# Window attention with MLP and GDN: value projection and value copies moved ahead of the turns, and another strip for odd halves

## The chip, the cores and the metric

One core of a Trainium2 chip runs the whole program. The metric is the device time of one execution in microseconds (us). TensorE (PE in the rows) multiplies matrices, VectorE (DVE) and ScalarE (ACT) do elementwise work, GpSimd (POOL) some more of it, SyncE (SP) issues the transfers by DMA. Each engine works through its own list of instructions in order; semaphores make one wait for another.

## What is computed

The input x is 4 images of 96 channels and 128 x 128 points. The reference is a shifted-window transformer block followed by a generalised divisive normalisation:

```
y   = layernorm(x) over channels, rolled by (-4, -4), cut into windows of 8 x 8 = 64 tokens
q, k, v = y @ qkv_w.T + qkv_b, in 6 heads of 16
out = softmax(q k^T / 4 + mask) v @ proj_w.T + proj_b, windows put back, rolled by (4, 4)
x   = x + out
x   = x + gelu(layernorm(x) @ mlp_w1.T + mlp_b1) @ mlp_w2.T + mlp_b2
out = x * rsqrt(gamma_eff @ x^2 + beta_eff) over channels
```

The mask (-100) concerns the windows that the roll has wrapped: the last window of each row of windows, and all windows of the last row of an image.

## The kernel before

A unit is a row of 16 windows (8 image rows, 1024 tokens); there are 64 units. Each is worked on in two halves of 8 windows, so there are 128 halves, A = 0 to 127; the odd half of a unit holds windows 8 to 15, and so the masked last window. A half has four pairs of windows (pair 3 is LAST). All engines run the same pipeline of rounds H: in each round the stage of a step works on half H + offset. TURN_IN = 4 and TURN_OUT = 3 prepare later halves, QK = 1 and ATTEND = 0 are attention, PROJECT = -2, MLP = -3, UP = -4, SETTLE = -5 and DIVIDE = -6 are the steps behind it. The order of the steps in a round is written out by hand in one function `steps` for each engine.

Layout. Many tiles have 96 channels or heads as three groups of 32 partitions; partitions 96 to 127 are a fourth strip. So that all 128 partitions work on 384 columns (MAIN) instead of 96 on 512, the fourth pair's columns of the three groups are laid side by side in the strip. `in_strips` does a projection in this way: three matmuls of 384 columns for the main pairs, three of 128 for the strip.

One round on TensorE, for the half H of attention: `scores(H)` (four row groups; the strip's scores, group GROUPS = 3, go to pv_bank, the others to the three score_banks), `project_k` and `project_q` of H+1, `times_v(H-1)` (probabilities times values, into pv_bank), `denominators(H-6)`, `sum_probs(H-1)`, `project(H-2)`, `mlp_down(H-5)`, then `turn_run(H)`: the turns (transposes) of the probabilities of H, mixed with those of the normalised tokens y1 of H+3 and y2 of H-3 into turn_banks; then `project_v(H)` (8 matmuls of 96 columns into pv_bank), `mlp_up` parts 0 and 1 of H-4, `turn_in` of x for H+4 and of x2 for H-2 (turned to tokens, into turn_banks), `mlp_up` part 2.

VectorE: maxima and shifts of the scores (the strip's group first, then 0, 1, 2, with maxima and shifts interleaved), `normalise` for y1 and y2, `first_residual`, `divide(H-1)` (reads pv_bank, writes attended), `second_residual`, `outputs`, `split_y2(H-3)` (the rounding rest of y2), `v_blocks(H)` (four copies from pv_bank to v_block), `statistics` of x and x2 out of turn_banks, `variances`. ScalarE: table load, copies of k and q, the exponentials, with logarithms and inverses between them, table load, `y2_copy`, `y1_copy` out of turn_banks, then copies of the turned probabilities and gelus. SyncE issues the loads of x, the stores, and moves between strip and groups (`move_attended`, three transfers a half).

pv_bank is used in turn by the strip's scores of H, by times_v of H-1, and by project_v of H. The waits that matter around the change:

```
times_v(A):   pe.wait_ge(scores_shifted, softmax_count(A + 1, GROUPS))
project_v(A): wait(pe, attended_ready, A)
turn_in(A):   wait(pe, y_ready[0], min(H + TURN_OUT + 1, HALVES))
              wait(pe, y2_split, min(H + MLP + 1, HALVES))
split_y2(A):  dve.wait_ge(y_ready[1], A + 1), and y_ready[0] of the same round
scores(A):    waits for probs_t_ready and v_ready of the half before, q_ready, keys_copied
```

mlp_up part 2 waits for the gelu of part 0, whose bank of PSUM it takes over. The masks are added by matmuls of 4 rows (L1045) behind the scores of the window pair they belong to.

Of the kernel before, what the change touches and what calls it, by code (L numbers as in the profile page):

```python
# [32 lines left out]
HALF = UNIT // 2  # L33
HALVES = 2 * UNITS
HALF_WINDOWS = WINDOWS // 2
# [32 lines left out]
def window_block(nc, x, qmask, kmask, ident, head_mask, ones_pair, norm1_w, norm1_b, qkv_t, qkv_b,  # L68
# [8 lines left out]
    with ctx:  # L77
# [151 lines left out]
        def wait(engine, semaphore, count):  # L229

            if count > 0:
                engine.wait_ge(semaphore, count)
# [26 lines left out]
        def mm_bank(name, A):  # L259
            return mm_banks[MM_PLACE[name, A] % len(mm_banks)]  # L260
# [43 lines left out]
        def norm_round(A, ln):  # L304

            return A - (TURN_OUT, MLP)[ln]

        SOFTMAX_ORDER = (GROUPS, 0, 1, 2)

        def softmax_count(A, g):  # L310
# [3 lines left out]
        def group(j, width=32):  # L314
            return slice(width * j, width * (j + 1))
# [7 lines left out]
        def _(sp):  # L323
# [46 lines left out]
            def move_attended(A):  # L370

                wait_alone(sp, attended_ready, A + 1)
                for j in range(HEAD_PAIRS):
                    sp.dma_start(attended[group(j), MAIN:HALF], attended[strip, group(j, 128)])\
                        .then_inc(attended_moved, 16)

            def move_x3(A):
# [125 lines left out]
        def _(act):  # L503
# [55 lines left out]
            def softmax_exp(A, g):  # L559
                act.wait_ge(scores_shifted, softmax_count(A, g))  # L560
                for bank in ((0, 1, 2) if g == GROUPS else (0, 1) if g < 2 else (2,)):
                    wait(act, probs_turned[bank], A)
                dst = probs[:, :, LAST, :, :] if g == GROUPS else probs[:, g, 0:LAST, :, :]
                nc.scalar.activation(dst, shifted[:, g, :, :].rearrange("t (i e) k -> t i e k", e=TILE_HEADS),  # L564
                                     ACT.Exp).then_inc(probs_ready, 1)

# [70 lines left out]
        def _(dve):  # L637
# [166 lines left out]
            def divide(A):  # L804
                dve.wait_ge(inv_sum_ready, A + 1)
                dve.wait_ge(pv_made, A + 1)
                wait(dve, proj_made, A)
                nc.vector.tensor_tensor(attended[:, 0:MAIN], pv_bank[:, 0:MAIN], inv_sum[:, :],
                                        ALU.mult).then_inc(attended_ready, 1)

            def first_residual(A):
# [22 lines left out]
            def steps(run, H):  # L834

                run(max_scores, ATTEND, GROUPS)
                run(shift_scores, ATTEND, GROUPS)
                run(max_scores, ATTEND, 0)
                run(max_scores, ATTEND, 1)
                run(shift_scores, ATTEND, 0)  # L840
                run(max_scores, ATTEND, 2)
                run(shift_scores, ATTEND, 1)
                run(shift_scores, ATTEND, 2)
                run(normalise, TURN_OUT, 0)
                run(normalise, MLP, 1)
                run(first_residual, PROJECT)
                run(divide, ATTEND - 1)
                run(second_residual, SETTLE)
                run(outputs, DIVIDE)
                run(split_y2, MLP)  # L850
                run(v_blocks, ATTEND)
                run(statistics, TURN_IN, 0)
                run(statistics, PROJECT, 1)
                variances(H)
                if H == -TURN_IN:
                    fold_qkv()
                if H == -TURN_IN + 1:
                    fold_mlp()
                if H == -TURN_IN + 2:
                    split_mlp()  # L860
# [5 lines left out]
        def _(pe):  # L866
# [80 lines left out]
            def turn_run(H):  # L947
# [30 lines left out]
                for p in range(PAIRS):  # L978
                    if has(norm2):
                        turn_normed(norm2, 1, p, 0)  # L980
                    if has(A):
                        made = turn_windows(A, 2, p, 1)
                        if p == PAIRS - 1:
                            made.then_inc(probs_turned[2], 1)

            def project_k(A):

                if A == 0:
                    pe.wait_ge(weights_folded, 10)
                    pe.wait_ge(cleared, 2)  # L990
                pe.wait_ge(y_ready[0], A + 2 - A % 2)
                mm_wait("k", A)
                in_strips(mm_bank("k", A), wk, y1_windows(A, 0, 2 * LAST), y1_windows(A, 2 * LAST))\
                    .then_inc(k_made, 1)

            def project_q(A):

                pe.wait_ge(y_ready[0], A + 2 - A % 2)
                mm_wait("q", A)
                in_strips(mm_bank("q", A), wq, y1_windows(A, 0, 2 * LAST), y1_windows(A, 2 * LAST))\  # L1000
                    .then_inc(q_made, 1)

            def project_v(A):

                wait(pe, attended_ready, A)
                for p in range(PAIRS):
                    made = nc.tensor.matmul(pv_bank[:, p * DIM:(p + 1) * DIM], y1_windows(A, 2 * p, 2 * p + 2),  # L1007
                                            wv[:, :], start=True, stop=True)
                made.then_inc(v_made, 1)
# [5 lines left out]

            def window_of(A, r, i, n):

                return (A % 2) * HALF_WINDOWS + 2 * (LAST if r == GROUPS else i) + n

            def scores(A):  # L1020

# [28 lines left out]
            def times_v(A):  # L1050

                pe.wait_ge(v_ready, A + 1)
                pe.wait_ge(probs_t_ready, GROUPS * (A + 1))
                if has(A + 1):
                    pe.wait_ge(scores_shifted, softmax_count(A + 1, GROUPS))
                for turn in range(2 * LAST):
                    at, n = turn // 2, turn % 2
                    first = turn * TOKENS
                    for s in range(STRIPS):
                        m, p = (s, at) if s < HEAD_PAIRS else (at, LAST)  # L1060
                        made = nc.tensor.matmul(pv_bank[group(s), first:first + TOKENS],  # L1061
                                                v_block[:, (A % 2) * HALF_WINDOWS + 2 * p + n, m, :],
                                                probs_t[:, A % 2, m, p, n * TOKENS:(n + 1) * TOKENS],
                                                start=True, stop=True)
                made.then_inc(pv_made, 1)

            def sum_probs(A):

                if has(A + 1):
                    pe.wait_ge(scores_shifted, softmax_count(A + 1, 0))  # L1070
                for m in range(HEAD_PAIRS):
                    nc.tensor.matmul(sum_bank[group(m), 0:MAIN], ones_pair_sb[:, :],
                                     probs_t[:, A % 2, m, 0:LAST, :], start=True, stop=True)
                for m in range(HEAD_PAIRS):
                    made = nc.tensor.matmul(sum_bank[strip, group(m, 128)], ones_pair_sb[:, :],  # L1075
                                            probs_t[:, A % 2, m, LAST, :], start=True, stop=True)
                made.then_inc(sums_made, 1)

            def project(A):
# [40 lines left out]
            def steps(run, H):  # L1120
# [6 lines left out]
                run(sum_probs, ATTEND - 1)  # L1127
                run(project, PROJECT)
                run(mlp_down, SETTLE)
                turn_run(H)  # L1130
                run(project_v, ATTEND)
                run(mlp_up, UP, 0)
                run(mlp_up, UP, 1)
                run(turn_in, TURN_IN, 0)
# [62 lines left out]
```

## Time and profile before

| | before |
|---|---|
| median of 3 runs | 1757.68 us (1756.24 to 1758.75) |
| the profiled execution, its own time | 1756.11 us |
| span of its trace | 1754.3 us |
| TensorE busy (matmul / weight load) | 1662.1 us (95%) / 1464.1 us (83%) |
| ScalarE busy | 1487.8 us (85%) |
| VectorE busy | 1423.0 us (81%) |
| GpSimd busy | 361.1 us (21%) |
| granted TensorE clock, mean | 0.991 of full speed |
| the chain that ended last, by engine | PE 71%, DVE 17%, issue 5%, ACT 5% |

The busy shares are means over the whole span. A matmul is pipelined: the next one starts before it ends, so the pace of a row of matmuls is read from start to start. The chain is followed back from the last instruction, at each step to what released it.

### The profile page before, as it was taken

The numbers are of one execution on the slowest core, as the hardware profiler recorded it, in microseconds if no ns is written. First come the engines' busy times: TensorE is split into PE (matmuls) and PEld (weight loads), VectorE is DVE, ScalarE is ACT, GpSimd is POOL, SyncE is SP. The second block draws the span as 40 slices with busy tenths as digits, with TensorE's granted clock in tenths as the row PEclk, the third lists the DMA queues.
The fourth block names the chain that finished last, engine by engine and source line by source line (L and its number), as shares of the span: only waits on it lengthen the run. The fifth ranks groups of instructions, "written<-read, shape, count | busy, mean of one in ns | idle before, by whom it ended". The sixth has DMA issues, their size and how long they took to land.

```text
span 1754.3 us, 83088 instructions
## 1 busy us (share of the span) xinstructions
PE 1662.1 (95%) x33524; PEld 1464.1 (83%) x33524; DVE 1423.0 (81%) x4142; ACT 1487.8 (85%) x2957; POOL 361.1 (21%) x459
## 2 busy tenths in 40 slices
PE   5899999999999999999999999999999999999995
PEld 3688888888888888888888888888888888888874
DVE  5788888888888888888888888888888888888871
ACT  2688888888888888888888888888888888888884
POOL 2121221221221221221221221221222222222111
PEclk9999999999999999999999999999999999999997
DMA  2112122122122122122122122122121222222111
GB/s 57 47 51 64 55 61 62 54 64 59 55 61 62 54 61 62 54 67 57 54 69 56 53 68 57 53 68 57 55 66 56 56 66 57 57 64 57 46 34 32
DMA packets 179169, 100.38 MB, mean 57 GB/s; under 512 B 26868, under 2 KB 178790, under 8 KB 178790
## 3 DMA queue, kind: packets, MB, share of 16 engines
q1 hardware_dynamic: 178228, 94.96, 19.5%
q8 instruction: 269, 4.41, 1.1%
q14 instruction: 110, 0.90, 0.2%
q10 hardware_dynamic: 562, 0.11, 0.0%
HBM read 32.05 MB, written 25.17 MB: 33 GB/s over the span
## 4 chain that ended last, share of the span: by engine, by line
PE 71%; DVE 17%; issue 5%; ACT 5%; DMA 1%; SPq 0%; POOL 0%; DVEq 0%; POOLq 0%
PE mm_bank L906 10%; PE mm_bank L1111 10%; PE mm_bank L1096 8%; PE score_banks L936 7%; PE pv_bank L1061 6%; PE mm_bank L904 6%; DVE stats L721 5%; PE mm_bank L1108 5%; PE pv_bank L1007 4%; DVE v_block L783 4%; PE turn_banks L942 4%; PE score_banks L1075 3%; PE score_banks L1037 3%; DVE row_max L792 2%; DVE shifted L799 2%
## 5 line engine op out<-in xcount | busy, mean ns | idle before, releaser
L514 ACT ACT_TABLE_LOAD x256 | 328.4, 1283 | 4.6
L564 ACT ACTIVATE probs<-shifted 128x384 f32<-128x384 f32 x512 | 265.7, 519 | 32.0 <-DVE shifted L799 29.0
L1108 PE MATMUL mm_bank<-hidden,w 128*32 128x384 f32 x2304 | 277.4, 492 | 0.1
L1111 PE MATMUL mm_bank<-hidden,w 128*32 128x128 f32 x2304 | 276.8, 275 | 0.0
L593 ACT ACTIVATE hidden<-mm_bank 128x512 f32<-128x512 f32 x384 | 238.4, 621 | 42.2 <-PE mm_bank L1096 41.5
L1111 PEld LDWEIGHTS mm_bank<-hidden,w 128*32 128x32 f32 x2304 | 254.4, 111 | 1.2
L469 POOL TENSOR_TENSOR x<-x,b_bias 128x384 f32<-128x384 f32 x128 | 105.7, 826 | 716.7 <-PE turn_banks L928 716.7
L770 DVE TENSOR_TENSOR y_lo<-turn_banks,y_hi 96x512 fp32r<-96x512 f32 x128 | 87.9, 687 | 197.2 <-ACT y L538 194.3
L575 ACT ACTIVATE probs_t<-score_banks 128x512 f32<-128x512 f32 x384 | 220.1, 617 | 0.0
L792 DVE TENSOR_REDUCE row_max<-score_banks 128x6 f32<-128x384 f32 x384 | 199.4, 547 | 0.0
L799 DVE TENSOR_TENSOR shifted<-score_banks,row_max 128x384 f32<-128x384 f32 x384 | 199.3, 546 | 0.0
L721 DVE BATCH_NORM_STATS2 stats<-turn_banks 128x6 f32<-128x96 f32 x1024 | 181.7, 249 | 17.1 <-PE turn_banks L923 11.2
L783 DVE COPY v_block<-pv_bank 64x192 f32<-64x192 f32 x512 | 180.4, 352 | 11.7 <-PE pv_bank L1007 6.5
L936 PE MATMUL score_banks<-ident_sb,probs 64*128 64x64 f32 x3072 | 181.8, 229 | 4.0 <-ACT probs L564 2.3
L1096 PE MATMUL mm_bank<-y_hi,w_hi 97*128 97x512 f32 x384 | 172.9, 450 | 0.1
L936 PEld LDWEIGHTS score_banks<-ident_sb,probs 64*128 64x128 f32 x3072 | 146.5, 138 | 30.0 <-issue 24.4
L1061 PEld LDWEIGHTS pv_bank<-probs_t,v_block 128*32 128x32 f32 x6144 | 97.2, 110 | 74.6 <-issue 74.1
L1061 PE MATMUL pv_bank<-probs_t,v_block 128*32 128x64 f32 x6144 | 114.3, 221 | 44.4 <-DVE shifted L799 40.5
L1096 PE MATMUL mm_bank<-y_lo,w_hi 97*128 97x512 f32 x384 | 152.0, 396 | 0.0
L1096 PE MATMUL mm_bank<-y_hi,w_lo 97*128 97x512 f32 x384 | 150.6, 392 | 0.0
L1037 PE MATMUL pv_bank<-k_block,q 32*64 32x128 f32 x1536 | 147.5, 284 | 0.0
L1007 PE MATMUL pv_bank<-wv,y 97*128 97x96 f32 x1024 | 145.8, 286 | 0.0
(110 smaller groups left out, 4568.1 us busy)
## 6 DMA issues: line engine op xcount, KB each, us to landing
x_ext<-in_x SPq DMA_DIRECT2D x128, 192.0 KB, 3.2
k_block<-k SPq DMA_DIRECT2D x256, 96.0 KB, 2.0
out<-o_ext SPq DMA_DIRECT2D x64, 192.0 KB, 2.8
x_ext<-in_x SPq DMA_DIRECT2D x128, 48.0 KB, 2.8
attended<-attended SPq DMA_DIRECT2D x384, 16.0 KB, 1.8
x<-x SPq DMA_DIRECT2D x384, 16.0 KB, 1.8
out<-o_ext SPq DMA_DIRECT2D x64, 96.0 KB, 2.6
out<-o_ext SPq DMA_DIRECT2D x128, 48.0 KB, 2.1
```

Source lines behind the costliest of these rows:

```text
L514: nc.scalar.preload_act_table_set(name)
L564: nc.scalar.activation(dst, shifted[:, g, :, :].rearrange("t (i e) k -> t i e k", e=TILE_HEADS), ACT.Exp).then_inc(probs_ready, 1)
L593: nc.scalar.activation(hidden[:, n, :], mm_bank(f"mlp1_{n}", A)[:, :], ACT.Gelu)\
L721: made = nc.vector.bn_stats(stats[:, (H + 1) % 2, ln, n, :], chunk)
L783: made = nc.vector.tensor_copy(to, values[:, :, :, e, :])
L792: nc.vector.tensor_reduce(row_max[:, g, :], group_scores(g), op=ALU.max, axis=AX.X)\
L799: nc.vector.tensor_tensor(shifted[:, g, :, :], group_scores(g), row_max[:, g, :].unsqueeze(2) .broadcast_to([128, LAST * TILE_HEADS, TOKENS]),
L936: return nc.tensor.transpose(score_banks[:, bank, first:first + TOKENS], probs[half, m, p, :, :], ident_sb[half, half])
L1061: made = nc.tensor.matmul(pv_bank[group(s), first:first + TOKENS], v_block[:, (A % 2) * HALF_WINDOWS + 2 * p + n, m, :], probs_t[:, A % 2, ...
L1096: made = nc.tensor.matmul(mm_bank(f"mlp1_{n}", A)[:, :], w[:, cols], tokens, start=part == 0, stop=part == 2)
L1108: nc.tensor.matmul(to[group(j), 0:MAIN], w2[:, n, group(j)], hidden[:, n, 128:HALF], start=first, stop=last)
L1111: made = nc.tensor.matmul(to[strip, group(n, 128)], w2[:, c, group(n)], hidden[:, c, 0:128], start=c == 0, stop=c == HID_CHUNKS - 1)
```

## The change

On TensorE `project_v` is run before `turn_run` instead of behind it, and it also waits for the shift of the strip's scores of its own half. On VectorE `v_blocks` is run before `split_y2` instead of behind it. And the pair of windows that is laid in the fourth strip is no longer pair 3 in every half: in odd halves it is pair 0, and the three main pairs are 1 to 3 (`main_pairs`, `side_pair`). Slices that followed from the old choice follow from the new one: the columns of attended, the slices of the probabilities, the windows of q and k, the places of the masks.

```diff
@@ -305,6 +305,22 @@
+        def main_pairs(A):
+            return range(A % 2, A % 2 + LAST)
+        def side_pair(A):
+            return 0 if A % 2 else LAST
+        def main_tokens(A):
+            return slice(A % 2 * 128, A % 2 * 128 + MAIN)
+        def side_tokens(A):
+            return slice(side_pair(A) * 128, side_pair(A) * 128 + 128)
         SOFTMAX_ORDER = (GROUPS, 0, 1, 2)
...
@@ -371,7 +387,8 @@
                 for j in range(HEAD_PAIRS):
-                    sp.dma_start(attended[group(j), MAIN:HALF], attended[strip, group(j, 128)])\
+                    first = main_tokens(A).start + 128 * j
+                    sp.dma_start(attended[group(j), side_tokens(A)], attended[strip, first:first + 128])\
                         .then_inc(attended_moved, 16)
...
@@ -560,7 +577,8 @@
                     wait(act, probs_turned[bank], A)
-                dst = probs[:, :, LAST, :, :] if g == GROUPS else probs[:, g, 0:LAST, :, :]
+                pairs = slice(main_pairs(A)[0], main_pairs(A)[-1] + 1)
+                dst = probs[:, :, side_pair(A), :, :] if g == GROUPS else probs[:, g, pairs, :, :]
                 nc.scalar.activation(dst, shifted[:, g, :, :].rearrange("t (i e) k -> t i e k", e=TILE_HEADS),
...
@@ -805,7 +823,7 @@
                 wait(dve, proj_made, A)
-                nc.vector.tensor_tensor(attended[:, 0:MAIN], pv_bank[:, 0:MAIN], inv_sum[:, :],
+                nc.vector.tensor_tensor(attended[:, main_tokens(A)], pv_bank[:, 0:MAIN], inv_sum[:, :],
                                         ALU.mult).then_inc(attended_ready, 1)
...
@@ -847,8 +865,8 @@
                 run(outputs, DIVIDE)
+                run(v_blocks, ATTEND)
                 run(split_y2, MLP)
-                run(v_blocks, ATTEND)
                 run(statistics, TURN_IN, 0)
...
@@ -983,6 +1001,11 @@
+            def qk_windows(A):
+                side = 2 * side_pair(A)
+                return y1_windows(A, 2 * main_pairs(A)[0], 2 * main_pairs(A)[-1] + 2), y1_windows(A, side, side + 2)
             def project_k(A):
...
@@ -990,18 +1013,19 @@
                 mm_wait("k", A)
-                in_strips(mm_bank("k", A), wk, y1_windows(A, 0, 2 * LAST), y1_windows(A, 2 * LAST))\
+                in_strips(mm_bank("k", A), wk, *qk_windows(A))\
                     .then_inc(k_made, 1)
...
                 mm_wait("q", A)
-                in_strips(mm_bank("q", A), wq, y1_windows(A, 0, 2 * LAST), y1_windows(A, 2 * LAST))\
+                in_strips(mm_bank("q", A), wq, *qk_windows(A))\
                     .then_inc(q_made, 1)
...
+                pe.wait_ge(scores_shifted, softmax_count(A, GROUPS))
                 wait(pe, attended_ready, A)
...
@@ -1015,7 +1039,7 @@
-                return (A % 2) * HALF_WINDOWS + 2 * (LAST if r == GROUPS else i) + n
+                return (A % 2) * HALF_WINDOWS + 2 * (side_pair(A) if r == GROUPS else main_pairs(A)[i]) + n
...
@@ -1057,7 +1081,7 @@
                     for s in range(STRIPS):
-                        m, p = (s, at) if s < HEAD_PAIRS else (at, LAST)
+                        m, p = (s, main_pairs(A)[at]) if s < HEAD_PAIRS else (at, side_pair(A))
                         made = nc.tensor.matmul(pv_bank[group(s), first:first + TOKENS],
...
@@ -1070,10 +1094,10 @@
                     nc.tensor.matmul(sum_bank[group(m), 0:MAIN], ones_pair_sb[:, :],
-                                     probs_t[:, A % 2, m, 0:LAST, :], start=True, stop=True)
+                                     probs_t[:, A % 2, m, main_pairs(A)[0]:main_pairs(A)[-1] + 1, :], start=True, stop=True)
                 for m in range(HEAD_PAIRS):
                     made = nc.tensor.matmul(sum_bank[strip, group(m, 128)], ones_pair_sb[:, :],
-                                            probs_t[:, A % 2, m, LAST, :], start=True, stop=True)
+                                            probs_t[:, A % 2, m, side_pair(A), :], start=True, stop=True)
                 made.then_inc(sums_made, 1)
...
@@ -1127,8 +1151,8 @@
                 run(mlp_down, SETTLE)
+                run(project_v, ATTEND)
                 turn_run(H)
-                run(project_v, ATTEND)
                 run(mlp_up, UP, 0)
...
```

## Rows read from the trace of the kernel before

**Rows 1.** Busy time of each engine in an even and an odd round.

```profile
core 0: us, PE busy (x) PEld busy (x) DVE busy (x) ACT busy (x) POOL busy (x), PEclk, DMA share, GB/s
803.50:816.60 13.10, 12.43 (x259) 11.01 (x258) 10.99 (x32) 11.68 (x24) 3.74 (x5) 1.00 0.24 66
816.60:829.70 13.10, 13.03 (x265) 11.61 (x264) 10.98 (x32) 11.52 (x24) 1.82 (x2) 1.00 0.20 58
```

**Rows 2.** Matmuls of times_v (L1061) in 113 rounds: durations, first and last start.

```profile
L1061 PE MATMUL pv_bank<-probs_t,v_block x5424: 215/219/244, 156.2 to 1624.7; 128*32 128x64 f32 x194
```

**Rows 3.** Waits of the whole span: us in total, times, longest.

```profile
DVE y_lo L770 <- ACT y L538: 194.3, 122, 2.0
...
ACT y_hi L544 <- PE turn_banks L942: 75.3, 127, 1.2
...
ACT hidden L593 <- PE mm_bank L1096: 41.5, 130, 2.1
PE pv_bank L1061 <- DVE shifted L799: 40.5, 61, 1.3
ACT probs L564 <- DVE shifted L799: 29.0, 67, 1.0
```

**Rows 4.** Timeline of VectorE: start, us, line, operation, idle before.

```profile
802.82 0.54 DVE L808 TENSOR_TENSOR attended<-pv_bank,inv_sum 128x384 f32<-128x384 f32 x1
...
804.07 0.55 DVE L830 TENSOR_TENSOR o_ext<-x,inv_den 128x384 f32<-128x384 f32 x1
806.20 0.69 DVE L770 TENSOR_TENSOR y_lo<-turn_banks,y_hi 96x512 fp32r<-96x512 f32 x1 [1.58 <-ACT y L538]
806.80 1.45 DVE L783 COPY v_block<-pv_bank 64x192 f32<-64x192 f32 x4
808.28 1.42 DVE L721 BATCH_NORM_STATS2 stats<-turn_banks 128x6 f32<-128x96 f32 x8
...
811.12 0.56 DVE L799 TENSOR_TENSOR shifted<-pv_bank,row_max 128x384 f32<-128x384 f32 x1
...
819.30 0.69 DVE L770 TENSOR_TENSOR y_lo<-turn_banks,y_hi 96x512 fp32r<-96x512 f32 x1 [1.59 <-ACT y L538]
```

**Rows 5.** Timeline of ScalarE in the even round.

```profile
804.96 0.59 ACT L544 ACTIVATE y_hi<-turn_banks 96x512 fp32r<-96x512 f32 x1 [0.57 <-PE turn_banks L942]
...
806.93 0.62 ACT L593 ACTIVATE hidden<-mm_bank 128x512 f32<-128x512 f32 x1
```

**Rows 6.** Timeline of TensorE in the even round.

```profile
803.48 0.77 PE L936 MATMUL score_banks<-ident_sb,probs 64*128 64x64 f32 x17
...
804.73 0.22 PE L936 MATMUL score_banks<-ident_sb,probs 64*128 64x64 f32 x1
804.89 1.13 PE L1007 MATMUL pv_bank<-wv,y 97*128 97x96 f32 x8
805.80 0.48 PE L1096 MATMUL mm_bank<-y_hi,w_hi 97*128 97x512 f32 x1
...
807.28 0.49 PE L923 MATMUL turn_banks<-ident_sb,x_ext 96*128 96x96 f32 x4
...
807.86 0.47 PE L1096 MATMUL mm_bank<-y_hi,w_hi 97*128 97x512 f32 x1
...
808.72 0.35 PE L1037 MATMUL score_banks<-k_block,q 32*64 32x128 f32 x6
...
809.63 0.52 PE L904 MATMUL mm_bank<-y,wk 97*32 97x384 f32 x3
...
811.83 0.88 PE L1061 MATMUL pv_bank<-probs_t,v_block 128*32 128x64 f32 x48 [0.67 <-DVE shifted L799]
```

**Rows 7.** Timeline of TensorE in the odd round.

```profile
820.94 0.48 PE L1096 MATMUL mm_bank<-y_hi,w_hi 97*128 97x512 f32 x1
...
821.82 0.35 PE L1037 MATMUL score_banks<-k_block,q 32*64 32x128 f32 x6
...
823.32 0.52 PE L904 MATMUL mm_bank<-y,wk 97*32 97x384 f32 x3
...
824.91 0.31 PE L1061 MATMUL pv_bank<-probs_t,v_block 128*32 128x64 f32 x6
```

## The prediction

> **What bounds the kernel now.** I read the page first: no engine is idle for long, TensorE least of all. So the question is which loop of waits sets the length of a round, and the views of one pair of rounds tell it. The busy time of the two rounds from 803.5 to 829.7 us [rows 1] shows TensorE at 12.43 of 13.10 us in the even round and 13.03 in the odd one. The 113 rounds (5424 / 48 matmuls) in the middle of the trace have their first product with the values at 156.2 and their last at 1624.7 us [rows 2]: 1468.5 / 112 = 13.1 us a round, so these two stand for all. ScalarE works 11.68 and 11.52, VectorE 10.99 and 10.98. TensorE is full in odd rounds and has 0.67 us to spare in even ones.
>
> The list of waits [rows 3] says what that spare time is: in 61 rounds, one in two, TensorE waits at the products with the values (L1061) for VectorE's shifted scores, 40.5 us in all. VectorE waits 194.3 us for the copies of y (122 times, 1.59 us each) and ScalarE 75.3 us for the turns (127 times, 0.59 each). Put in order of time [rows 4 to 7], that is one loop through three engines. The last turn ends at 804.73 + 0.22 = 804.95. ScalarE starts at 804.96 with the copy of y2, then copies y1. VectorE, idle since 804.62, splits y2 from 806.20 to 806.89, copies the values (v_block, to 808.25), takes the statistics (808.28), the variances, the maximum and the shift of the fourth strip's scores (to 811.68). TensorE waits for that and starts times_v at 811.83, goes on through denominators, sums, project and mlp_down without a pause, and turns again. From the split's end to times_v it takes 811.83 - 806.89 = 4.94 us, and in the odd round 824.91 - 819.99 = 4.92. Both rounds are as long as this loop; the value projection (804.89) runs beside ScalarE's copies and is not on it.
>
> **The change, step by step.** *Loss: the value projection enters the loop.* project_v now stands between mlp_down and the turns. Its eight matmuls take 0.91 us from their first start to the first start of mlp_up behind them (804.89 to 805.80), and 1.13 from first start to last end [rows 6]. The turns, both copies of y and the split come later by something between these; I take the middle, 1.02. What could cover it is a wait that the turns now have, and I see none: they start right behind mlp_down (803.48), and ScalarE, the next in the loop, is waiting for them in each round.
>
> The rows also show what a change of tile costs on TensorE: from the last turn (64 rows) to the first value matmul (97 rows) 0.16 us pass from start to start. The Trainium skill (TensorEngine Tiling (Array Packing), Key Properties) has a rule that speaks against this change: going to another tiling mode drains the engine. Before, a round goes from 32-column tiles to 64-row turns to the whole array; afterwards to the whole array, back to the turns and to the whole array again, one switch more. By that rule with the row's 0.16 the loss would be 1.18 instead of 1.02; no row of this case shows the step from values to turns.
>
> *Its waits.* project_v now waits for the shift of the fourth strip (already met, since times_v waited for it) and, earlier than before, for the division of the half before, since both use pv_bank. The division ends at 802.82 + 0.54 = 803.36 [rows 4]; with the 0.15 us that TensorE took behind the shift (811.68 to 811.83) the values could start at 803.51, where the turns started at 803.48. So it costs nothing but has no slack: whatever is queued behind it on TensorE (turns, mlp_up, turn_in) and ScalarE's copies would be late with it.
>
> *Gain: the value copies leave the loop.* v_blocks now stands ahead of the split. The values are ready by about 803.48 + 1.13 = 804.61, VectorE's outputs end at 804.62, so the four copies (1.45 us) run from 804.65 to 806.1, while the split must wait until 806.20 + 1.02 = 807.22 in any case. VectorE's idle time hides them with 1.1 us to spare; without that they would hold up the split and the statistics queued behind it.
>
> But the statistics need more than VectorE: turn_in waits for the split (y2_split), and the statistics read what turn_in wrote. Before, turn_in (807.28 to 807.77) was done while VectorE copied values. Now it stands in the loop: split's end + 0.15 + the 0.49 of the first four turns + 0.01 (as ScalarE behind the last turn) = 0.65 after the split, where the statistics now start 1.39 after it (808.28 - 806.89). From the statistics to times_v nothing changes, 3.55. Split to times_v becomes 4.20 instead of 4.94: gain 0.74. The 0.15 is bounded by 0 and by the 0.39 that passed with TensorE still busy (806.89 to 807.28), so the gain by 0.50 and 0.89.
>
> *TensorE's own way to times_v* is now nearly as long. mlp_up's third part waits for the first gelu, which ends at 807.55 [rows 5], 0.66 after the split, + 0.15 = 0.81 after it (turn_in alone would let it start at 0.15 + 0.58 = 0.73). In an even round, from there 809.63 - 807.86 = 1.77 to the keys and 824.91 - 823.32 = 1.59 to times_v: 4.17, just under VectorE's 4.20. In an odd round the scores take 823.32 - 821.82 = 1.50, against 809.63 - 808.72 = 0.91 in an even one [rows 6, 7]: 0.59 for the mask matmuls, which stand in one row group.
>
> *The strip.* Taking pair 0 as the strip of odd halves moves the masked last window from the strip to the three main pairs, so its three masks fall on three row groups instead of one. Number and shape of matmuls, copies, exponentials and moves by DMA stay. Between nothing and all of the 0.59 can be saved; I take two thirds, 0.39, because three row groups share it (the scores of four groups already overlap: 48 matmuls in 0.91). The odd way becomes 0.81 + (824.91 - 820.94) - 0.39 = 4.39 instead of 4.92: 0.53 gained. With nothing saved 4.78 (0.14 gained), with all of it 4.19, and VectorE's 4.20 decides.
>
> *ScalarE* gets the turns 1.02 later but times_v only 0.3 to 0.5 later, so its softmax comes late by 0.5 to 0.7 against TensorE. It has 0.30 of wait before the third gelu (41.5 us in all) and 0.44 before an exponential (29.0 us) to take that up [rows 3]; I put the rest at nothing.
>
> *Sum.* Even round 1.02 - 0.74 = +0.28; odd 1.02 - 0.53 = +0.49; mean 0.385. The loop with all its parts stands in halves 3 to 123, 121 rounds (before that there is no y2, after it no turn_in of x); the few others I leave out. 121 x 0.385 = 47 us. The profiled execution took 1756.1, so 1803; the median of the runs is 1.6 higher, so 1805. By bounds: 0.91 - 0.89 in even and 0.91 - 0.73 in odd rounds give +12 us (1770), 1.13 - 0.50 and 1.13 + 0.10 give +113 (1870) if every bound is bad at once.
>
> **Rivals.**
> *Covered values (faster).* If part of the value projection falls into time in which the turns would have waited anyway, the loss is smaller. From 0.385 of the 1.02 on the kernel gets faster; fully covered, a round loses 0.635, 77 us: 1681, which TensorE's 12.43 a round (and 13.03 - 0.39 in odd ones) just allows; half covered 1743. Against it stands ScalarE's wait for the turns in 127 rounds. For it: VectorE's gain of 0.74 in every round is sure, and an earlier split would follow at once. Chance 0.10.
> *Balance.* A cover of about 0.385 or the kindest bounds: within 0.2% (3.5 us, about what a measurement of this kernel can tell from no change), 1757. Chance 0.04.
> *The division is late.* project_v has no slack behind it. If ScalarE's lateness reaches the inverse sums and so the division by 0.2 us, each round grows by that: 24 us more, 1829. It decides from the first 0.03 us on. Chance 0.08.
> *One more change of tile.* From the 0.16 of the row, another 121 x 0.16 = 19 us: 1824. Chance 0.08. It is the skill's rule above.
> *The masks don't spread.* Odd rounds +0.88, mean 0.58: 1828. Here the strip part would do nothing for the time. Chance 0.06.
>
> **The numbers.** The sum as worked out has a chance of 0.64, with its own range 1785 to 1820. The slower rivals end between 1824 and 1829, together 0.22; the faster 0.10; balance 0.04. The range 1770 to 1830 takes in the sum, most of the slower ones and the kind bounds, and leaves out the faster case. Slower by over 0.2%: 0.86; within: 0.04; faster: 0.10.
>
> **What would show it.** In the profile after: rounds of about 13.4 and 13.6 us; the value copies at once behind the outputs and VectorE idle between them and the split; TensorE idle by some 0.6 us before turn_in, waiting for the split, and the wait before times_v gone or small; the statistics 0.65 after the split; odd scores in about 1.1 us. I am wrong if the turns start less than 0.6 us later after mlp_down, or if turn_in doesn't wait for the split.

## The result, and the profile after

The changed kernel takes 1870.13 us in the median of 4 runs (1868.95 to 1872.21), the kernel before 1756.96 (1756.02 to 1758.75): ratio 1.0643, 95% interval 1.0628 to 1.0658, 113 us more. The forecast was 1805 with a range to 1830. The sign was right, the size was not.

VectorE's timeline over one round after (columns as in [rows 4]):

```profile
863.61 0.69 DVE L788 TENSOR_TENSOR y_lo<-turn_banks,y_hi 96x512 fp32r<-96x512 f32 x1 [1.16 <-ACT y L555]
...
874.35 0.55 DVE L848 TENSOR_TENSOR o_ext<-x,inv_den 128x384 f32<-128x384 f32 x1
874.94 1.46 DVE L801 COPY v_block<-pv_bank 64x192 f32<-64x192 f32 x4
877.54 0.69 DVE L788 TENSOR_TENSOR y_lo<-turn_banks,y_hi 96x512 fp32r<-96x512 f32 x1 [1.15 <-ACT y L555]
878.94 1.42 DVE L739 BATCH_NORM_STATS2 stats<-turn_banks 128x6 f32<-128x96 f32 x8 [0.70 <-PE turn_banks L941]
880.46 0.81 DVE L752 TENSOR_TENSOR mean_gap<-stats 128x8 f32<-128x8 f32 x1
881.18 0.16 DVE L754 TENSOR_TENSOR within<-stats 128x8 f32<-128x8 f32 x1
...
882.25 0.56 DVE L817 TENSOR_TENSOR shifted<-pv_bank,row_max 128x384 f32<-128x384 f32 x1
```

A round now lasts 877.54 - 863.61 = 13.93 us. The value copies stand right behind the outputs, in idle time, as forecast; the split still waits for ScalarE's copies; the statistics start 878.94 - 878.23 = 0.71 after its end, 1.39 before. The row that matters is mean_gap, the first instruction of the variances: 0.81 us for 8 elements on each partition, where the three instructions behind it, of the same size, take 0.16 and 0.17. GpSimd's timeline in the same round shows bias_x2, which adds a bias to x2, and the square of x3, which the denominators need:

```profile
879.41 0.83 POOL L486 TENSOR_TENSOR x<-x,b_bias 128x384 f32<-128x384 f32 x1 [9.44 <-PE turn_banks L946]
880.19 1.04 POOL L493 TENSOR_TENSOR x_sq<-x 96x512 f32<-96x512 f32 x1
```

The square (x_sq) runs until 880.19 + 1.04 = 881.23, and mean_gap ends at 881.27. The same two rows of the kernel before, VectorE first, then GpSimd:

```profile
809.80 0.33 DVE L734 TENSOR_TENSOR mean_gap<-stats 128x8 f32<-128x8 f32 x1
```

```profile
808.28 0.83 POOL L469 TENSOR_TENSOR x<-x,b_bias 128x384 f32<-128x384 f32 x1 [2.99 <-PE turn_banks L928]
809.07 1.03 POOL L476 TENSOR_TENSOR x_sq<-x 96x512 f32<-96x512 f32 x1
```

There the square ended at 810.10 and mean_gap at 810.13, after 0.33. In the 114 rounds in the middle of each trace mean_gap ends 0.03 us behind the square, but for one round after. TensorE's timeline after, to be read against [rows 6, 7]:

```profile
873.79 1.11 PE L1031 MATMUL pv_bank<-wv,y 97*128 97x96 f32 x8
874.83 0.77 PE L954 MATMUL score_banks<-ident_sb,probs 64*128 64x64 f32 x17
...
876.08 0.22 PE L954 MATMUL score_banks<-ident_sb,probs 64*128 64x64 f32 x1
876.23 0.50 PE L1120 MATMUL mm_bank<-y_hi,w_hi 97*128 97x512 f32 x1
...
878.38 0.52 PE L941 MATMUL turn_banks<-ident_sb,x_ext 96*128 96x96 f32 x4 [0.48 <-DVE y_lo L788]
...
882.96 0.88 PE L1085 MATMUL pv_bank<-probs_t,v_block 128*32 128x64 f32 x48 [0.36 <-DVE shifted L817]
```

The values stand ahead of the turns (873.79), turn_in waits for the split, 0.48 us idle before it, and times_v waits for the shift in this even-to-odd round and, as the waits show, in nearly all others (114 instead of 61 in [rows 3]):

```profile
ACT y_hi L561 <- PE turn_banks L960: 214.2, 127, 3.9
DVE y_lo L788 <- ACT y L555: 140.9, 122, 1.8
...
DVE stats L739 <- PE turn_banks L941: 102.3, 128, 3.6
...
PE turn_banks L941 <- DVE y_lo L788: 61.0, 121, 2.1
...
PE pv_bank L1085 <- DVE shifted L817: 50.5, 114, 1.3
...
ACT probs L582 <- DVE shifted L817: 35.9, 114, 1.0
```

ScalarE now waits 214.2 us for the turns instead of 75.3 (1.69 a round instead of 0.59), which is the later turns; VectorE waits for turn_in in 128 rounds, where it did in 4 before, and TensorE for the split, where it did not.

**The loop in numbers.** Medians over the middle rounds of each trace, first matmul of times_v to that of the next round:

| piece of the loop, us | before | forecast | after |
|---|---|---|---|
| times_v to the y2 copy | 6.22 | 7.24 | 7.29 |
| y2 copy to the split's end | 1.93 | 1.93 | 1.93 |
| split's end to the statistics | 1.40 | 0.65 | 0.71 |
| statistics to times_v | 3.53 | 3.55 (odd rounds 3.74, TensorE's way) | 4.02 |
| round | 13.09 | 13.37 and 13.58 | 13.94 |

Most of the miss within a round is in the fourth row (0.47 of 0.57 us in even rounds, 0.28 of 0.36 in odd ones), and there mean_gap alone is 0.48 us longer (0.32 before, 0.81 after). The rest of the 113 us is in the first rounds: times_v of half 4 comes 10.8 us later than before, and from there to half 123 the distance grows by (113.3 - 10.8) / 119 = 0.86 a round. The busy time of stretches of 20 us there shows TensorE's granted clock below full speed (the last but two column) for longer, after first, then before. At 1.00 it is at the upper of its two levels, 2.4 GHz, and at 0.50 at the lower, 1.2 GHz; by these shares it spent some 27 us at the lower one after and 14 before. In the stretch ahead of the fall after, TensorE was busy for 14.69 of 20 us:

```profile
20.00:40.00 20.00, 14.69 (x160) 11.37 (x156) 10.86 (x38) 7.80 (x21) 3.43 (x4) 1.00 0.15 45
40.00:60.00 20.00, 16.14 (x318) 13.81 (x322) 11.66 (x33) 7.65 (x20) 1.71 (x2) 0.83 0.16 44
60.00:80.00 20.00, 15.68 (x257) 13.55 (x248) 12.90 (x37) 8.23 (x21) 1.03 (x2) 0.71 0.16 47
80.00:100.00 20.00, 15.54 (x284) 12.75 (x284) 12.99 (x44) 12.57 (x27) 3.16 (x3) 0.78 0.05 14
```

```profile
20.00:40.00 20.00, 13.78 (x162) 10.92 (x158) 9.46 (x32) 7.81 (x21) 3.43 (x4) 0.89 0.15 45
40.00:60.00 20.00, 16.32 (x342) 14.06 (x344) 14.17 (x41) 9.72 (x25) 1.72 (x2) 0.77 0.17 50
60.00:80.00 20.00, 15.22 (x368) 13.03 (x368) 16.54 (x53) 11.14 (x28) 3.36 (x4) 1.00 0.19 52
80.00:100.00 20.00, 19.11 (x337) 16.47 (x329) 15.53 (x45) 17.33 (x35) 1.14 (x3) 1.00 0.15 44
```

That the clock accounts for the 10.8 us is not shown. With the new strip alone (below) TensorE spent some 4 us at the lower level (0.91 from 40 to 60 us, 1.00 else), 10 less than the kernel before, and yet times_v of half 4 came 0.5 us later than there. Another part is in the waits: four times in these rounds, 7.5 us in all, TensorE waits for the division ahead of the value projection, which it never did in the kernel before.

### The profile page after: what moved, and what is told of

Its sections match the earlier page's. It is cut to its first block, busy times and chain, and to the rows that moved or that the text cites. A ratio compares the mean times of both kernels' runs of the same rounds, so it can differ in the third digit from the quotient of the medians.

```text
span 1870.4 us, 83215 instructions
## 1 busy us (share of the span) xinstructions
PE 1699.6 (91%) x33524; PEld 1449.3 (77%) x33524; DVE 1493.3 (80%) x4142; ACT 1484.9 (79%) x2957; POOL 360.2 (19%) x459
## 3 DMA queue, kind: packets, MB, share of 16 engines
q8 instruction: 270, 4.42, 1.0%
## 4 chain that ended last, share of the span: by engine, by line
PE 58%; DVE 27%; ACT 9%; issue 5%; DMA 1%; SPq 0%; POOL 0%; DVEq 0%; POOLq 0%; ACTq 0%
PE mm_bank L1135 9%; DVE stats L739 8%; PE pv_bank L1031 7%; PE mm_bank L924 7%; PE score_banks L954 6%; PE pv_bank L1085 6%; DVE mean_gap L752 5%; PE mm_bank L1132 5%; DVE y_lo L788 5%; ACT y_hi L561 4%; PE mm_bank L922 4%; ACT y L555 4%; PE turn_banks L941 4%; PE turn_banks L960 4%; DVE shifted L817 3%
## 5 line engine op out<-in xcount | busy, mean ns | idle before, releaser
L561 ACT ACTIVATE y_hi<-turn_banks 96x512 fp32r<-96x512 f32 x128 | 75.9, 593 | 214.4 <-PE turn_banks L960 214.2
L1031 PEld LDWEIGHTS pv_bank<-wv,y 97*128 97x128 f32 x1024 | 124.7, 192 | 33.5 <-issue 33.1
```

## The experiments

Round lengths are medians as above, even and odd rounds apart where they differ. Times are medians; each ratio is to runs of the kernel before on the same chip. The theory called *lock* in the expectations is that VectorE's mean_gap is held until an instruction of GpSimd ends.

**Is it GpSimd's square? (1) Square 8 of 512 columns.**

```diff
...
-  nc.gpsimd.tensor_tensor(x3_sq[0:DIM, :], x3[0:DIM, A % 2, :], x3[0:DIM, A % 2, :], ALU.mult)
+  nc.gpsimd.tensor_tensor(x3_sq[0:DIM, 0:8], x3[0:DIM, A % 2, 0:8], x3[0:DIM, A % 2, 0:8], ALU.mult)
...
```

The rest of x3_sq is set to 1 once at the start, so this kernel leaves the other 504 columns out of the denominators.

> The changed kernel, but GpSimd squares 8 of the 512 columns of x3 (the denominators then lack the rest). Theory (lock): mean_gap, which reads two tiles of SBUF, is held until GpSimd's square ends; with the square gone it takes about 0.17 us instead of 0.81, split to times_v falls from 4.72 to about 4.1 or 4.2, where TensorE's own way decides: 0.5 to 0.6 us a round, 1795 to 1810 us. Rival (late turns): the loss comes from the turns alone and the long mean_gap only fills time in which TensorE isn't ready: mean_gap may get short, the time stays at 1865 to 1875.

Measured 1817.26 us, ratio 1.0334 (1.0317 to 1.0352): 53 us come back. The group of mean_gap by form (count, busy us, mean ns), with the square small and in the changed kernel:

```profile
L753 DVE TENSOR_TENSOR mean_gap<-stats 128x8 f32<-128x8 f32 x122 | 21.1, 173 | 12.7
```

```profile
L752 DVE TENSOR_TENSOR mean_gap<-stats 128x8 f32<-128x8 f32 x122 | 95.1, 779 | 12.7
```

173 instead of 779 ns. Split to times_v falls from 4.73 to 4.09 and 4.25, as the theory had it, rounds to 13.45 and 13.47 in the median (undisturbed even ones 13.30); the time ends 7 us above the range named, because 42 of the 111 rounds are longer by over 0.15 us than the 13.30 and 13.47 of their kind (below). The time fell with mean_gap, so late turns alone don't explain the loss.

**(2) The square ahead of bias_x2, nothing left out.**

```diff
-                run(bias_x2, PROJECT)
                 run(square, SETTLE)
+                run(bias_x2, PROJECT)
```

> The changed kernel with GpSimd's square ahead of bias_x2 instead of behind it, nothing left out. Theory (lock): the square runs while VectorE waits for the split or takes statistics, bias_x2 ends before mean_gap begins, mean_gap takes about 0.17: again 1795 to 1810 us. Rival (late turns): 1865 to 1875. If the moved strip of x3 lands later than assumed, the square delays bias_x2 into mean_gap and the time lies between.

1825.25 us, 1.0375 (1.0360 to 1.0391): between the two, nearer to the lock. mean_gap takes at most 0.20 in 90 rounds and longer in 24.

**(3) The square waits for the variances.** It stays behind bias_x2, which ends before mean_gap starts in nearly all rounds, so neither should hold it:

```diff
                 wait_alone(pool, den_made, A)
+                wait_alone(pool, spread_ready, min(spread_count(A - SETTLE), spread_count(HALVES - 1 - PROJECT)))
```

> The changed kernel, GpSimd's square waits for the variances. Theory (lock, and late moves of x3 made the rounds with the square ahead or small uneven): mean_gap 0.17 in all rounds; split to times_v 4.1 and 4.25 by TensorE's own way; rounds of 13.3 and 13.47, a mean loss of 0.3 us in 119 rounds and 10 us in the first ones: 1798 to 1808 us. Rival (the uneven rounds have another cause): 1815 to 1830.

1820.50 us, 1.0358 (1.0342 to 1.0373). mean_gap takes 0.17 in all rounds, split to times_v 4.09 and 4.25, rounds 13.30 and 13.47 as expected. With all of the work done and mean_gap free, the time is 50 us below the changed kernel's. But the mean round is 13.55, so 0.16 x 111 = 18 us lie in longer rounds, which the late move of x3 does not explain: there, and with its time, the rival holds. TensorE's timeline in one of the longer rounds:

```profile
992.51 0.64 PE L1086 MATMUL pv_bank<-probs_t,v_block 128*32 128x64 f32 x29
993.63 0.47 PE L1086 MATMUL pv_bank<-probs_t,v_block 128*32 128x64 f32 x18 [0.48 <-issue]
993.89 0.51 PE L923 MATMUL mm_bank<-x_sq,wgdn 97*32 97x384 f32 x3
```

Within the 48 matmuls of times_v TensorE sat for 0.48 us with nothing to wait for that the profile shows. The page of this run counts the transfers that load instructions (270 packets, 4.42 MB):

```profile
q8 instruction: 270, 4.42, 1.1%
```

One of these (16 KB each) ends at 992.44, 1.20 us before TensorE's weight loads resume at 993.63. In 93 rounds of this trace 29 weight loads start over 0.15 us later behind the load before than is usual at their place, 11.5 us in all, and 23 of these, 10.4 us, start 1.0 to 1.8 us behind the end of such a transfer; chance would give one in eight. The kernel before has 2 such gaps in 94 rounds. So the long rounds go with the loading of instructions. That it causes them is not shown, since no run varies it.

**The strip alone.** The new strip with both orders of before.

```diff
-                run(project_v, ATTEND)
                 turn_run(H)
+                run(project_v, ATTEND)
...
-                run(v_blocks, ATTEND)
                 run(split_y2, MLP)
+                run(v_blocks, ATTEND)
```

> The kernel before with the strip of odd halves from pair 0, the order of before. Theory (loop): the loop through VectorE decides in odd rounds too, so the shorter scores (about 1.1 instead of 1.5 us) turn into wait before times_v: 1750 to 1759 us, no change. Rival (TensorE is full in odd rounds and decides there): 0.39 us in 61 rounds, 24 us, 1733.

1756.56 us, 0.9989 (0.9980 to 0.9999): no change by the 0.2% named in the prediction. The odd scores take 1.10 us instead of 1.50, and times_v waits in 119 rounds instead of 61. The loop through VectorE decides in both rounds.

**The orders alone.** The kernel before with project_v and v_blocks moved and pair 3 in the strip of all halves.

> The kernel before with project_v ahead of the turns and v_blocks ahead of the split, the strip as before. Theory (lock): VectorE's way of 4.72 us from split to times_v hides the masks but for 0.06 us, so 1868 to 1880 us. Rival (masks count once TensorE starts late): 0.39 us more in 61 odd rounds, 1894.

1875.79 us, 1.0673 (1.0651 to 1.0695), against 1.0643 with the strip. The rounds are the same 13.93 in the median. Of the 11 us by which its profiled execution is longer than the changed kernel's (1883.1 and 1872.2), 4 lie ahead of half 4 and 5 are spread over the rounds from there to half 123. With the strip alone worth nothing, the whole loss belongs to the orders.

**The value projection ahead, the value copies not.**

```diff
-                run(v_blocks, ATTEND)
                 run(split_y2, MLP)
+                run(v_blocks, ATTEND)
```

> The changed kernel with v_blocks behind the split again; project_v stays ahead of the turns, the strip stays changed. Theory (the loss is the 1.06 us by which the turns come later, the value copies out of the loop win only the 0.21 that mean_gap's hold leaves): rounds of 13.09 + 1.06 = 14.15, mean_gap 0.32 as before, 1885 to 1900 us. Rival (the move of the value copies is what hurts): faster than the changed kernel's 1870.

1880.23 us, 1.0691 (1.0675 to 1.0707), 5 us below the range named. Rounds of 14.00, not 14.15, since mean_gap takes 0.17 here: with the statistics as late as 1.40 after the split, the square has only 0.08 us left when mean_gap starts, less than mean_gap needs by itself. So the lock was not as before, which I had assumed; the rest is as expected.

**The kernel before with the lock off.** First with the square ahead of bias_x2, without and with the new strip:

> The kernel before with GpSimd's square ahead of bias_x2. Theory (lock): the kernel before pays for the lock too, its mean_gap takes 0.32 us and ends 0.03 after the square; with the square ahead it takes 0.17. The loop through VectorE falls from 13.09 to 12.94 us, in odd rounds TensorE's 13.0 decides: 0.1 us a round, 1740 to 1750 us. Rival (the lock bites only in the changed order): 1754 to 1760.

1754.46 us, 0.9983 (0.9973 to 0.9992).

> The same with the strip of odd halves from pair 0, order of the turns as before. Theory (lock and loop): with the odd scores shorter by 0.4 both rounds follow VectorE's loop, 12.94 us: 0.15 x 121 = 18 us, 1734 to 1744. Rival (the strip never counts): as the run without the strip, within 3 us.

1753.62 us, 0.9972 (0.9960 to 0.9984). Both times miss the theory's ranges and lie where the rivals had put them, though the median round is 12.95 in both, as the theory had it; the mean round is 13.07 and 13.08. VectorE's and GpSimd's timelines of the second show why:

```profile
821.81 0.42 DVE L752 TENSOR_TENSOR mean_gap<-stats 128x8 f32<-128x8 f32 x1
...
834.99 0.69 DVE L752 TENSOR_TENSOR mean_gap<-stats 128x8 f32<-128x8 f32 x1
...
848.45 0.17 DVE L752 TENSOR_TENSOR mean_gap<-stats 128x8 f32<-128x8 f32 x1
```

```profile
820.38 1.04 POOL L493 TENSOR_TENSOR x_sq<-x 96x512 f32<-96x512 f32 x1 [8.70 <-PE turn_banks L946]
821.38 0.82 POOL L486 TENSOR_TENSOR x<-x,b_bias 128x384 f32<-128x384 f32 x1
...
833.83 1.04 POOL L493 TENSOR_TENSOR x_sq<-x 96x512 f32<-96x512 f32 x1 [3.52 <-DMA x<-x]
834.83 0.82 POOL L486 TENSOR_TENSOR x<-x,b_bias 128x384 f32<-128x384 f32 x1
...
846.17 1.04 POOL L493 TENSOR_TENSOR x_sq<-x 96x512 f32<-96x512 f32 x1 [7.85 <-DMA x<-x]
847.17 0.82 POOL L486 TENSOR_TENSOR x<-x,b_bias 128x384 f32<-128x384 f32 x1
```

Where the square starts late, bias_x2 behind it runs into mean_gap: 821.38 + 0.82 = 822.20 against 821.81 + 0.42 = 822.23, 835.65 against 835.68. It isn't the square as such but any of the two that is under way. With the square behind the variances instead (the edit of (3)) and the new strip:

> The kernel before with the new strip, and GpSimd's square waits for the variances, still behind bias_x2. Theory (the last two runs with the square ahead had rounds of 12.95 us in the main, but a square that waited for a late move of x3 ran into mean_gap in the others): with the collision excluded all rounds take 12.95, 1735 to 1745 us. Rival (the long rounds have another cause): 1750 to 1757.

1742.16 us, 0.9912 (0.9895 to 0.9928), rounds of 12.94, mean 12.96, mean_gap 0.17 in all: 0.9% faster than the kernel before. Against the strip alone (1756.56) it is 14 us, which is what the lock cost in that order.

**Turns of y first.** The 16 turns of y1 and y2 ahead of the 24 of the probabilities, square ahead of bias_x2; in the order of before with the new strip, then in the changed order.

```diff
...
+                for r in range(2):
+                    for p in range(PAIRS):
+                        if has(norm1):
+                            turn_normed(norm1, 0, p, r)
+                        if has(norm2):
+                            turn_normed(norm2, 1, p, 1 - r)
                 if has(A):
                     wait(pe, log_sum_made, A)
...
```

> The same, and the turns of y1 and y2 run ahead of those of the probabilities, value projection and value copies where they were before. Theory (loop): only the turns of y stand in the loop; they end some 0.8 us earlier, ScalarE can use 0.57 of it (its wait for the turns), then TensorE's 12.4 and 12.6 us decide: rounds of 12.5 to 12.7, 1690 to 1715 us. Rival (all turns are needed before the loop goes on): 1734 to 1744.

1756.72 us, 0.9991 (0.9982 to 1.0000), above both ranges. The y2 copy does start earlier (5.66 after times_v instead of 6.22), but the value projection behind the turns starts 0.44 later (6.59 instead of 6.15): unmixed, the turns take 1.69 us from the first start to the last instead of 1.25, and rounds stay at 12.95 and 12.90 in the median, 13.10 in the mean.

> The changed kernel with the square ahead of bias_x2 and the turns of y ahead of those of the probabilities. Theory (the value projection costs because it stands ahead of the turns of y): the loop of 13.4 us falls by the 0.8 us that the turns of the probabilities take, to 12.6, TensorE decides, and the first rounds keep their 10 us: 1705 to 1725 us. Rival (the value projection ahead costs wherever the turns stand): 1780 or more.

1786.67 us, 1.0169 (1.0156 to 1.0183), rounds of 13.14 and 13.09: the rival's range (1780 or more) held. With the turns of y first, the value projection ahead of them still costs 30 us (1756.72 without).

**The variances later.** VectorE's variances behind the shift of the strip's scores, bias_x behind them:

```diff
                 run(shift_scores, ATTEND, GROUPS)
+                variances(H - 1)
...
-                variances(H)
...
-                    wait_alone(pool, max_ready, SCORE_GROUPS * (A - TURN_IN + 1) + 1)
+                    wait_alone(pool, spread_ready, spread_count(A - TURN_IN))
```

> The kernel before with the new strip; VectorE's variances run behind the shift of the fourth strip's scores instead of ahead of its maximum, and GpSimd's bias_x waits for them instead of for the maximum. Theory (loop through VectorE): 0.8 us less between split and times_v, mean_gap meets no GpSimd work, TensorE's 12.4 and 12.6 us decide: 1690 to 1710 us. Rival (ScalarE or another wait holds the round at 12.9 or more): 1735 to 1757.

1743.57 us, 0.9920 (0.9902 to 0.9938). times_v no longer waits, but sum_probs now does, for the shift of group 0, which the variances have pushed back (33.8 us in 96 rounds). The rival held.

> The changed kernel with the variances behind the shift and bias_x waiting for them. Theory (lock off the path; then TensorE's way from the split, 4.1 and 4.25 us, and the 1.06 us of value projection ahead of the turns decide): rounds of 13.35 and 13.47, 1795 to 1815 us, so the changed order still loses to the kernel before. Rival (the lock was the whole loss): 1757 or less.

1881.00 us, 1.0698 (1.0682 to 1.0714): above both theories. mlp_down ends 5.36 after times_v instead of 4.82 and the y2 copy comes 7.85 after it instead of 7.29. One more step puts the variances behind the shift of group 0, and ScalarE's rstd behind the exponential of group 0:

```diff
                 run(shift_scores, ATTEND, 0)
+                variances(H - 1)
...
-                rstd_pair(H)
                 run(softmax_exp, ATTEND, 0)
+                rstd_pair(H)
```

> The kernel before with the new strip; the variances behind the shift of group 0 (so that sum_probs doesn't wait for them), ScalarE's rstd behind the exponential of group 0, bias_x behind the variances. Theory (with the variances out of VectorE's way to both waits, TensorE's own time decides): rounds of 12.4 and 12.6 us, 1680 to 1705 us. Rival (another wait of TensorE on VectorE or ScalarE takes over, as sum_probs did): 1735 to 1757.

1716.19 us, 0.9762 (0.9745 to 0.9778): the fastest version here, in the order of before. Rounds are 12.76 and 12.58, and the busy times of two of them show TensorE as the bound:

```profile
core 0: us, PE busy (x) PEld busy (x) DVE busy (x) ACT busy (x) POOL busy (x), PEclk, DMA share, GB/s
803.50:829.00 25.50, 25.37 (x563) 22.23 (x563) 21.10 (x64) 22.84 (x46) 5.57 (x7) 1.00 0.22 62
```

It misses its range because mlp_down now ends 5.08 us after times_v instead of 4.82, and because 22 of 111 rounds are longer than these by over 0.15 us, which adds some 11 us to the time.

> The changed kernel with the same three edits. Theory (neither lock nor shift on the path; what stays is the 1.06 us of value projection ahead of the turns against 0.7 to 0.8 us won behind the split): rounds of 13.3 to 13.5, 1795 to 1810 us. Rival (TensorE's order itself is no loss): at most 1757.

1879.12 us, 1.0693 (1.0677 to 1.0709), no faster than the changed kernel, so this theory fell. The waits name what took over:

```profile
PE pv_bank L1031 <- DVE attended L826: 34.2, 110, 2.1
```

```profile
PE pv_bank L1031 <- DVE attended L826: 7.5, 4, 2.2
```

With the variances ahead of it on VectorE, the division of the half before comes later, and the value projection, which now stands ahead of the turns, waits for it in 110 rounds, 0.31 us each (4 in the changed kernel); mlp_down ends 0.26 later here too. So the y2 copy comes 7.85 after times_v instead of 7.29.

## Why the prediction was wrong

**The step that failed** is "From the statistics to times_v nothing changes, 3.55". It became 4.02, because the duration of mean_gap in it did not stay. mean_gap subtracts one part of stats from another, so both its inputs are in SBUF; GpSimd's bias_x2 and square read SBUF too. Where one of these is under way as mean_gap starts, mean_gap ends 0.03 us behind it: behind a square that starts late or early, and behind bias_x2. Where neither overlaps it, or less than its own 0.17 us of theirs is left, it takes 0.17. The one exception among the middle rounds of the changed kernel shows the hold on another instruction, VectorE's rows first, then GpSimd's:

```profile
517.67 0.17 DVE L752 TENSOR_TENSOR mean_gap<-stats 128x8 f32<-128x8 f32 x1
517.76 1.02 DVE L754 TENSOR_TENSOR within<-stats 128x8 f32<-128x8 f32 x1
```

```profile
517.70 1.05 POOL L493 TENSOR_TENSOR x_sq<-x 96x512 f32<-96x512 f32 x1
```

mean_gap started 0.03 ahead of the square and was free; within, which also reads two parts of stats, took 1.02 instead of 0.16 and ended 0.03 behind the square (518.78 and 518.75).

Earlier statistics brought mean_gap forward against the split; but turn_in, which releases bias_x2 and so the square, now starts 0.56 us ahead of the statistics instead of 1.00 (807.28 and 808.28 in [rows 4, 6]; 878.38 and 878.94 after). So mean_gap starts 1.05 us behind bias_x2 instead of 1.52 and meets 0.5 us more of GpSimd's pair. The prediction goes through what the earlier copies would hold up on VectorE and TensorE, and says nothing of GpSimd. The mean_gap of before, 0.33 where the next took 0.16, was the row that told of it.

The Trainium skill (SBUF — State Buffer, Who interferes with whom) states this: GpSimd and VectorE share one pair of ports, held for a whole instruction, and a VectorE instruction with two SBUF inputs contends with a GpSimd instruction that reads SBUF. The 0.03 us by which mean_gap ends behind the square agrees, and so do VectorE's instructions that read PSUM: the statistics take 0.25 us each beside GpSimd's instruction (427 of them in the middle rounds after) as without it (216).

**Four runs with the new strip put the rest in order.** Order of before without the lock: 12.94 a round, 1742 us. Value projection ahead, no collision: 14.00, 1880. Value copies ahead too, no collision: 13.39, 1820. The changed kernel, with it: 13.94, 1870. So:

- *Loss 1.02*: 14.00 - 12.94 = 1.06. Right, and not covered by anything; the covered rival is out. The values' first start to the first turn is 874.83 - 873.79 = 1.04, against 0.91 to mlp_up in [rows 6]: 0.13 more with the step to the turns. The Trainium skill (TensorEngine Tiling (Array Packing), Key Properties) says that a change of tiling mode drains the engine. The 0.13 agrees with such a cost, but no run separates it from other causes; it is inside the 1.06 and no second loss.
- *Gain 0.74 (0.53 in odd rounds)*: 14.00 - 13.39 = 0.61 with the lock off, of which statistics that start 0.70 earlier are the source and TensorE's own way the limit. Right but for size. With the lock, 0.06.
- *TensorE's own way, 4.17 and 4.39*: 4.09 and 4.25 once VectorE no longer decides. Right to 0.14; in the changed kernel hidden behind 4.73.
- *The strip, 0.39 of 0.59*: 1.50 - 1.10 = 0.40. Right, and worth nothing in the time, since VectorE's way decides in both rounds.
- *The division has no slack*: the value projection waited for it in the first rounds of the changed kernel alone (4 times, 7.5 us), and in 110 rounds as soon as VectorE had the variances ahead of it.
- *"The few others I leave out"*: by half 4 they cost 10.8 us. The value projection's waits for the division and some 27 us at the lower clock level instead of 14 fall into these rounds; which share belongs to which is open.

Sum: 47 us forecast, + 121 x (0.85 - 0.385) = 56 for the lock and the small errors, + 11 for the first rounds = 114, against 113 measured. By run (3) the lock itself is 50 of the 65 us by which the time passed the forecast of 1805; without it the time, 1820.50, lies in the range. That the prediction's worst bounds also add up to 113 us is chance: the terms that they stretch came out well inside, the loss at 1.06, the step behind the split at 0.15 and the strip at 0.40. Neither of its signs of being wrong appeared (the turns start 1.06 us later, and turn_in waits for the split); of what was to be seen, the round lengths and the wait before times_v, gone or small, are what failed. Of the range: it held bounds for TensorE and VectorE only, and no case in which a duration taken from before changes because another engine's work moves onto it. One sum of the rivals is off: with the values fully covered, rounds of 13.09 - 0.635 = 12.46 would be shorter than the 12.54 that TensorE's 12.43 and 13.03 - 0.39 come to in the mean, so 1681 was out of reach.

## What to carry to other kernels

When a step moves, list what each instruction will run beside on the engine that shares its ports, not only what it waits for: the stretched mean_gap counts as busy time (95.1 us over the span, 21.1 in run (1)) and stands in no list of waits. An instruction much longer than its twin of the same shape, ending together with one of another engine, is the sign; look for it before pricing anything "unchanged". And taking work out of a loop is worth only what remains after the work that was hidden beside it (here turn_in) and the work that had to go in (here the value projection) are counted.

## What was not expected of the hardware

- A VectorE subtraction of 128 x 8 elements took 0.16 to 0.17 us free and up to 0.81 beside GpSimd, with its end 0.03 us behind GpSimd's instruction in 113 of 114 rounds.
- With mean_gap free, 37 of 111 rounds stayed longer by 0.1 to 1.0 us, one by 2.1, and most gaps in them end 1.0 to 1.8 us behind a transfer that loads instructions. In the changed kernel, whose times_v waits anyway, such rounds are few (15 of 111 differ from 13.9). That the transfers cause them is not shown.
